# Splitting the expert down product's weights ahead of time and running it as three float32r products

## The reference, cut to what matters

```python
E, TOP_K, H, I = (8, 2, 256, 704)
probs = jax.nn.softmax(x @ gate_w.T, axis=-1)
topk_vals, topk_idx = jax.lax.top_k(probs, TOP_K)
...
g = jnp.einsum('th,eih->tei', x, w1)
u = jnp.einsum('th,eih->tei', x, w3)
a = jax.nn.silu(g) * u
y = jnp.einsum('tei,ehi->teh', a, w2)
out = jnp.einsum('te,teh->th', combine, y)
```

## Time and profile before

| | |
|---|---|
| median of 3 runs | 578.97 us (578.96, 578.97, 583.65) |
| span of the profiled execution | 579.5 us |
| the profiled execution's own time | 581.32 us |
| PE, PEld busy | 88%, 72% of the span |
| DVE, ACT, POOL busy | 65%, 50%, 28% |
| mean granted PE clock | 0.957 of full speed |
| moved by DMA | 47.46 MB, mean 82 GB/s |

### The profile page before, as it was taken

The page is one execution under the profiler, slowest core; times in us unless marked ns, Lnnn a source line. Parts: engine busy times, 40 slices in busy tenths (PEclk is TensorE's granted clock), DMA queues, the critical chain, the costliest instruction groups (busy, mean ns, idle before and its releaser), DMA issues. The chain is left out here.

```text
span 579.5 us, 9940 instructions
## 1 busy us (share of the span) xinstructions
PE 512.8 (88%) x3274; PEld 418.7 (72%) x3275; DVE 377.1 (65%) x964; ACT 287.1 (50%) x528; POOL 161.3 (28%) x221
## 2 busy tenths in 40 slices
PE   1996988999999989889989999628999999999994
PEld 1645776787787866667777777517888888898883
DVE  4896666737554545777777878356677766666661
ACT  1477432314402345555566566326666666666651
POOL 3703423932012202433222202110322222222222
PEclk9998989999999995899899999958999999999999
DMA  9997002000000019500000003941211222222111
GB/s 339 393 335 226 2 1 74 0 1 0 1 16 22 1 38 418 221 18 30 29 10 19 29 1 117 402 123 28 32 28 34 36 36 36 36 36 36 27 17 20
DMA packets 25780, 47.46 MB, mean 82 GB/s; under 512 B 2192, under 2 KB 21136, under 8 KB 25360
## 3 DMA queue, kind: packets, MB, share of 16 engines
q1 hardware_dynamic: 21232, 41.35, 19.8%
q0 software_dynamic: 4080, 5.15, 5.8%
q10 hardware_dynamic: 432, 0.49, 0.3%
HBM read 32.01 MB, written 14.98 MB: 81 GB/s over the span
## 5 line engine op out<-in xcount | busy, mean ns | idle before, releaser
L1609 PE MATMUL ps<-split,xsT 128*128 128x352 f32 x552 | 95.5, 329 | 0.8 <-DVE split L1251 0.8
L1609 PEld LDWEIGHTS ps<-split,xsT 128*128 128x128 f32 x552 | 89.4, 192 | 1.0 <-issue 1.0
L1251 DVE TENSOR_TENSOR split<-early,split 128x1408 fp32r<-128x1408 f32 x46 | 72.6, 1618 | 1.9 <-ACT split L788 1.9
L1631 PE MATMUL ps<-mid,work 128*128 (+1 forms) x276 | 67.9, 387 | 0.8 <-ACT work L777 0.8
L788 ACT CAST split<-early 128x1408 fp32r x46 | 62.6, 1365 | 0.8 <-issue 0.8
L1631 PEld LDWEIGHTS ps<-mid,work 128*128 128x128 f32 (+1 forms) x276 | 49.6, 189 | 13.5 <-issue 8.7
L1232 DVE TENSOR_TENSOR work<-work,ps 128x704 f32<-128x704 f32 x23 | 20.4, 889 | 56.4 <-PE ps L1609 56.4
L1121 DVE TENSOR_REDUCE nmax<-ps 128x1 f32<-128x128 f32 (+7 forms) x64 | 45.4, 751 | 7.5 <-PE ps L1515 7.4
L568 POOL TENSOR_TENSOR rstd<-mhalf 128x1 f32<-128x1 f32 x23 | 11.4, 495 | 138.2 <-ACT work L784 138.2
L1526 PE MATMUL ps<-cst,work 128*128 128x128 f32 x216 | 35.7, 294 | 4.8 <-DVE work L1129 2.8
L733 ACT COPY work<-ps 128x128 f32<-128x128 f32 (+7 forms) x32 | 20.6, 643 | 33.9 <-PE ps L1526 33.8
(11 more groups left out here) (250 smaller groups left out, 1129.9 us busy)
## 6 DMA issues: line engine op xcount, KB each, us to landing
early<-m_w SPq DMA_DIRECT2D x16, 704.0 KB, 10.2
expert_in<-pad SPq DMA_DIRECT2D x8, 1040.0 KB, 12.6
mid<-m_w SPq DMA_DIRECT2D x8, 640.0 KB, 8.3
work<-expert_in SPq DMA_DIRECT2D x23, 130.0 KB, 2.5
early<-factors SPq DMA_DIRECT2D x1, 2048.0 KB, 12.2
early<-wq SPq DMA_DIRECT2D x1, 2048.0 KB, 16.6
mid<-f_w SPq DMA_DIRECT2D x1, 2048.0 KB, 21.0
rows<-x_in SPq DMA_DIRECT2D x2, 512.0 KB, 5.1
```

The source lines that it names most:

```text
L1251: V.tensor_tensor(lo, (ew1, ew3)[w][:, bass.ds(e, 1), :], hi.bitcast(F32), ALU.subtract).then_inc(s_wlo[w], 1)
L1609: last = mm(ps[:, 2 * w + a, 0:IH], xsT[px][b][:, k, :], split_w[w][pw][:, k, a * IH:(a + 1) * IH], start=(k == 0 and px == pw), stop=(k = ...
L1631: last = mm(ps[:, 6, 0:D], eaT[0:w, b, c, :], we[0:w, c, :], start=(c == 0), stop=(c == IB - 1))
```

## The change

**Down product.** It becomes three float32r products: 18 of 256 columns instead of 6 float32 ones. Its activation is split behind the transposes: ACT rounds 512 and 256 columns into `eaT[0]`, DVE subtracts them into `eaT[1]`, both in one buffer for all tiles.

**Weights `w2`.** They are split once for all experts in the feed-forward stage, in 16 pieces of 128 x 768. A piece is loaded into one of four buffers in `mid`, rounded by ACT, subtracted by DVE, and both parts are stored to DRAM. `W2_AT_BLOCK` and `W2_BETWEEN` say behind which block a piece is handled. At the end of attention the high parts of all experts are loaded into `mid` as before; the low part of one expert (768 KB) is loaded for each tile, two buffers.

**Up product.** The 1408 columns of `w1` and `w3` lie side by side and are made in products of 512, 512 and 384 columns, 18 a tile instead of 24. The semaphore on which silu and the rounding of the next `w1` wait comes after the second of the three blocks (it came after the first half), that for DVE's product after the third.

**Padding.** The weights get 768 rows, zeros in the last 64, and the activation 64 zero columns; all six chunks are full.

```diff
+W2_COLS = IB * D // 2
+W2_BUFS = 4
+W2_PIECES = 2 * E
...
+        W2_AT_BLOCK = {2: 0, 3: 1, 4: 2, 5: 3, 6: 4, 7: 5, 8: 10, 9: 11, 10: 12, 13: 13, 14: 14, 15: 15}
+        W2_BETWEEN = (6, 7, 8, 9)
...
+            def store_w2_piece(p):
+                e, half = divmod(p, 2)
+                sp.wait_ge(s_w2lo, p + 1)
+                for d, part in zip(w2_split_d, (w2_hi, w2_lo)):
+                    sp.dma_start(d[e * P:(e + 1) * P, half * W2_COLS:(half + 1) * W2_COLS],
+                                 part[p % W2_BUFS].bitcast(F32)).then_inc(s_w2st[p % W2_BUFS], 16)
+
+            sp.wait_ge(s_mo, TT)
+            for p in range(W2_BUFS):
+                load_w2_piece(p)
...
+            for p in range(W2_PIECES):
+                store_w2_piece(p)
+                if p + W2_BUFS < W2_PIECES:
+                    sp.wait_ge(s_w2st[p % W2_BUFS], 32 * (p // W2_BUFS + 1))
+                    load_w2_piece(p + W2_BUFS)
...
+            def load_ahead(i, b, first=False):
+                sp.wait_ge(s_ext, i + 1)
+                sp.wait_ge(s_dest, i + 1)
+                load_slots(i + 2, b)
+                if not first:
+                    sp.wait_ge(s_ey, i - 1)
+                    load_w2_lo(i, b)
...
+            def w2_piece_hi(p):
+                act.wait_ge(s_w2ld[p % W2_BUFS], 16 * (p // W2_BUFS + 1))
+                nc.scalar.copy(w2_hi[p % W2_BUFS], w2_raw[p % W2_BUFS]).then_inc(s_w2hi, 1)
+
...
                 if q == FB:
                     feature_major(PH_FFN, 1, C_LN2)
+                    for p in W2_BETWEEN:
+                        w2_piece_hi(p)
...
             feature_major(PH_ATT, 0)
+            for b in range(W2_BUFS):
+                act.wait_ge(s_w2st[b], 32 * W2_PIECES // W2_BUFS)
...
-                nc.scalar.copy(eaT[:, b, 0:4, :].rearrange("p a b -> p (a b)"), ps[:, 4, :]).then_inc(s_eaa, 1)
+                for c, w in ((0, 4), (4, 2)):
+                    nc.scalar.copy(eaT[0][:, c:c + w, :].rearrange("p a b -> p (a b)"),
+                                   ps[:, 4 + c // 4, 0:w * P]).then_inc(s_eah, 1)
...
+            def w2_piece_lo(p):
+                dve.wait_ge(s_w2hi, p + 1)
+                b = p % W2_BUFS
+                V.tensor_tensor(w2_lo[b], w2_raw[b], w2_hi[b].bitcast(F32), ALU.subtract).then_inc(s_w2lo, 1)
...
-            ffn_residual(range(GT))
+            for p in W2_BETWEEN[:2]:
+                w2_piece_lo(p)
+            for t in range(GT):
+                ffn_residual(range(t, t + 1))
+                if t < 2:
+                    w2_piece_lo(W2_BETWEEN[2 + t])
...
-                V.tensor_copy(eaT[:, b, 4, :], ps[:, 5, 0:P])
-                V.tensor_copy(eaT[0:ILAST, b, 5, :], ps[0:ILAST, 5, P:2 * P]).then_inc(s_ead, 1)
-
+                for n, (c, w) in enumerate(((0, 4), (4, 2))):
+                    dve.wait_ge(s_eah, 2 * i + n + 1)
+                    hi, lo = (a[:, c:c + w, :].rearrange("p a b -> p (a b)") for a in eaT)
+                    last = V.tensor_tensor(lo, ps[:, 4 + c // 4, 0:w * P], hi.bitcast(F32), ALU.subtract)
+                last.then_inc(s_eal, 1)
...
+                for a in range(3):
+                    if a < 2:
+                        pe.wait_ge(s_wlo[a], i + 1)
+                    c0, c1 = a * 512, min((a + 1) * 512, 2 * I)
+                    for k in range(KD):
+                        for px, pw in PARTS:
+                            last = mm(up_flat[:, c0:c1], xsT[px][b][:, k, :], split_w[pw][:, k, c0:c1],
+                                      start=(k == 0 and px == pw), stop=(k == KD - 1 and px == 1))
+                    if a:
+                        last.then_inc((s_eg, s_eu)[a - 1], 1)
...
+                pe.wait_ge(s_eah, 2 * i + 2)
+                pe.wait_ge(s_ew2lo[b], 8 * (i - b) + 16)
+                pe.wait_ge(s_eal, i + 1)
...
-                for c in range(IB):
-                    w = min(P, I - c * P)
-                    last = mm(ps[:, 6, 0:D], eaT[0:w, b, c, :], we[0:w, c, :], start=(c == 0), stop=(c == IB - 1))
+                we_split = (we, ew2_lo[b].rearrange("p (c n) -> p c n", c=IB))
+                for px, pw in PARTS:
+                    for c in range(IB):
+                        last = mm(ps[:, 6, 0:D], eaT[px][:, c, :], we_split[pw][:, c, :],
+                                  start=(c == 0 and px == pw), stop=(c == IB - 1 and px == 1))
```

More of the change, by code:

```diff
@@ L231, in build @@
         split_t = sb("split", 4 * KD * I, F32R)
-        split_w = [[view(split_t, (w * 2 + part) * KD * I, KD, I) for part in range(2)] for w in range(2)]
+        split_w = [view(split_t, part * 2 * KD * I, KD, 2 * I) for part in range(2)]
         xsT_t = sb("xsT", 4 * D, F32R)
@@ L1099, in _ @@
             normalise(PH_FAC, x, 1)
+            for b in range(W2_BUFS):
+                dve.wait_ge(s_w2st[b], 32 * W2_PIECES // W2_BUFS)
             for q in range(FILLS):
```

114 lines of the change are left out of this document (67 added, 47 removed).

## The result

The changed kernel takes **592.31 us** in the median of four runs (589.87 to 593.9); the kernel before has 579.14 (four runs, 578.96 to 583.65). The ratio is 1.0167 with a 95% interval of 1.0126 to 1.0207: slower by 1.3 to 2.1%. The median lies outside the forecast's 1% and 0.3 us above the upper end of the range (592). By the ratio it is 586.4 to 591.1 us where before has 579.14, which is inside the range; the two medians alone give 1.0227, above that interval, so the size of the loss is known to some 3 us only. The first rival, a slow ring with 588 us, is what happened.

The account below looks back on a forecast made before the run. PE was taken to bound the loop before, a chain through DVE and ACT after; 579.5 - 10.4 (loop) + 9.2 (ring) + 1.0 (clock) = 579.3, about 579 us, no change. Range 568 to 592 us; within 1% (573.2 to 584.8) had 0.45.

Parts of the forecast that it names:

- The first rival: Feed-forward stage: reads and stores in one queue hold each other up, cycle 5.5 us, 588 us; 0.33 together with an ungained loop.
- The loop: Tile loop: rounds fall from 7.64 to 7.1 us, a gain of 10.8 us over the 20 full rounds.
- a chain of 7.08 us: Tile loop: second up block, silu, rounding of the next w1, both low parts and handovers bound a round, not PE's 6.88.
- The two handovers of 0.1: Tile loop: estimated 0.1 us each for two handovers between DVE, ACT and PE; bound 7.3 us a round at 0.2 each.
- DVE's room: Tile loop: DVE has about 6.1 us of work in a 7.1 us round, so splitting the activation hides.
- Transfers in the loop and at the end of attention: A tile's low weights take 1.9 us plus a fixed part, the extra high weights 1.5 us; both hide.
- The pieces' own work: Feed-forward stage: a piece takes DVE 0.93 to 1.4 us and ACT 0.81, costed at nothing inside blocks of 2.8 us.
- The cycle of the ring: Feed-forward stage: SP's two stores, wait and load take 4.6 us a piece, bounds 3.8 and 5.4; second group 9.2 us later.
- the load's share: Feed-forward stage: the load issued just before, 0.94 to 1.2 us, may add from nothing to all of itself to each cycle.
- The steps behind the cycle: Feed-forward stage: late pieces delay the additions, 6 us per us of cycle; from 4.9 piece 14 leads, 11 us per us.
- The clock: Feed-forward stage: PE's wait of about 5 us for piece 7 lowers its clock, costing 1 us, bounds 0 and 3.
- PE at 1.2 GHz in the second group: Feed-forward stage: a sign named beforehand that would show the forecast wrong, PE running at reduced clock there.

Follow-up runs that it names:

- e6: Against the kernel before: e1 with the up product back in 24 products of 352 columns and semaphores at its halves; ratio 0.9724, rounds 6.85 us.
- e9: The change with SP storing the next piece before waiting, pieces respread, and the up product in 352 columns with semaphores at the halves; ratio to before 0.9738.
- e3: The change with only the low parts stored, one store a piece, high parts left unrounded; ratio to the kernel before 1.0009.
- e5: The change with the loads of pieces 4 to 15 issued by ACT, in another queue than SP's stores; ratio to the kernel before 1.0234.
- e4: The change with DVE's low parts of pieces 6 to 9 moved behind the first group's additions, statistics and normalised rows; ratio to before 1.0156.
- e2: The change with SP issuing the stores of piece p + 1 before waiting for those of piece p; ratio to the kernel before 0.9929.
- e7: The kernel before with the padding alone: 768 weight rows, six full chunks, still float32 products; ratio 0.9899, rounds 7.31 us.
- e11: The change's serial ring with 8 pieces of 1536 columns in two buffers, handled at other blocks; one run 582.52 us, before 583.27.
- e1: The change with only piece 0 loaded and split, its parts stored to all 16 places without waits between; ratio to the kernel before 0.9863.

## Why the forecast missed and what of it held

**The loop held.** Forecast was a chain of 7.08 us and rounds of 7.1, against 7.13; a gain of 10.8 us over 20 rounds, against 10.3. Each link is in the trace: from the second up block to silu 495.68 - 494.00 = 1.68 (1.41 + 0.24 forecast), 0.72 to the rounding (0.71), the rounding 1.37, both low parts 3.16 (3.15), the idle time ahead of the second block 0.24 (some 0.2). The two handovers of 0.1 and the 0.03 for a restarting PE had no row behind them; the trace has 497.91 - 497.77 = 0.14 from ACT's rounding to DVE's low part and 0.05 from there to PE. e6 shows that this chain, not PE, is the bound, and that PE's own round is 6.85 (6.88 forecast). The down product came to 2.13 us (2.14 forecast). DVE's room held as well: the activation's low part made no wait except at the last tile, where PE stood 2.13 us for it (0.82 before); the shorter last product was to pay for that and the tail came out 0.9 longer. The clock explains this, not the order: the last down product ran mostly at half clock, behind that wait.

```profile
580.02 1.57 PE L1719 MATMUL ps<-expert_w,eaT 128*128 x6 [2.13 <-DVE eaT L1352]
```

Its 18 products took 3.91 us from there, at a mean clock of 0.57, where the 12 of before took 3.05; in the profiled execution of e9 they took 2.42 at full clock behind a wait of 2.03, and the tail was 1.2 us shorter than before's (20.7 against 21.9).

**Transfers in the loop and at the end of attention held:** 4.3 us to landing for a low part, and no wait of PE for them. (The high weights are 512 KB more than before, 0.52 MB and not 0.6.)

**The pieces' own work held, with a caveat.** 0.93 to 1.4 for DVE, measured 1.49 to 1.50 for the first five, 0.94 to 0.96 for the others, and 1.12 on the mean; 0.81 for ACT, measured 0.84. e9 shows that it can be hidden, down to 0.4 us, but only once the pieces are ready in time.

**The cycle of the ring is the term that failed.** It was 4.6, "the middle" of 3.8 and 5.4, and is 5.55, above the upper bound. The lower part was close: 3.3 to 3.7 for the pair and 0.5 for an issue, measured 3.32 where no load runs and 0.38. The mis-sized term is the load's share: it was let in at 0 to 1.2 us, its bytes alone, and costs 1.85 in the change, 1.83 in e3 and 1.9 in e5. Choosing the middle made it worse: of the two ends, the upper had all three transfers in flight together, which is what the code does in every cycle, and the lower assumed that one of them was free. The rest of the 20 us followed from this term, at 6 to 11 us for each us of the cycle.

**The steps behind the cycle held, the last one by luck.** With 5.5 in place of 4.6 my formulas give piece 7's load at 107.1 + 22 - 0.5 = 128.6 (measured 128.21), piece 9's at 139.6 (139.13), and piece 14 rounded at 171.1 (171.90). But piece 14 is not what held the last silu:

```profile
172.83 0.60 ACT L763 ACTIVATE work<-ps 128x512 f32<-128x512 f32 x1 [0.92 <-PE ps L1521]
```

ACT waited for PE there. What led was piece 12: DVE handled it at 159.87, the product behind it came at 161.88, PE started again at 162.61 and then made the remaining blocks without a wait, 3.40 us of that time at half clock, which is 1.7 us lost. That this ended 0.9 us behind piece 14 is why the rival's delay of 17.1 + 2 for the clock comes so near to the 19.2 in the trace. (The two paths cross at c = 5.0 by the prediction's own terms, not 4.9.) It was right that from about 5 us on late pieces of the second group lead, and not the hold of the additions: e4 takes that hold away and gains 1.1 us at most. The rival's 588 us is the 588.8 that the ratio gives; the profiled span grew by 11.1 where the rival has 8.7, and the 2.4 between them are the 1.3 ahead of the loop, the 0.9 at the tail, and tenths.

**The clock** was put at 1 us with bounds of 0 and 3. PE had 13.6 us at half clock in the stage. The first 10.2 of them stood under waits for DVE, as argued: the next additions came at 144.46, when piece 9 let them, and PE stood another 2.92 us for DVE ahead of 151.18. The last 3.4 did not, and cost 1.7. Of the signs named beforehand as speaking against the forecast, "PE at 1.2 GHz in the second group" came true. The Trainium skill, "TensorE: Matmul & The Clock Gate", "Part 1: The HAM clock gate", says that an idle TensorE loses clock; PE's 8.95 us wait had it in its second half, and in e2's profiled execution, with no wait of PE in the stage above 1.9, the clock stayed at 1.00, so the trace agrees.

**A fixed part and a rate do not give the cycle either.** The Trainium skill, "DMA: Bandwidth & Descriptors", "Anatomy of one DMA — SWDGE (gpsimd) path", has about 2.0 us and 436 GB/s, for another queue than this. The estimate by it was c = 4.3 without the load; with all three transfers of a cycle in it, an estimate by it is 2.0 + 1.18 MB / 436 GB/s = 4.7 us. Both are under the measured 5.55, while its 3.8 for the pair of stores is above the measured 3.32: here the fixed part is smaller, about 1.4 us, and what is missing is the load's share beside the stores.

## What to carry to other kernels

Where a program stages data through DRAM in a ring of buffers, write down what is in flight while a landing is waited for. One that waits for each store before it issues the next pays the fixed part of a transfer in every cycle, and here a load in flight slowed the stores from whichever queue it came; issuing the next piece's stores ahead of the wait was worth 15 us of the stage here (12.6 to 13.8 us of the whole by the ratios), and no engine's work changed. A piece of work that is small and "fits into every block" still costs as much as its data is late, because the engine works in order: put it where the engine waits anyway, and see first that the data is there.

Undo one part of a change at a time before judging it: here the padding alone was worth 1.0%, the wide product nothing (and 0.28 us a round less than nothing together with the rest), and the split down product 1.6% of time (e9 against e7, with some 0.6 either way) once the ring stopped taking it back.

## What the runs showed of the hardware

- A pair of 393 KB stores is through in 3.32 us when alone and in 5.25 us when a load of 393 KB starts with it in another queue (e5); in the same queue the load's issue and its share add 2.2 us (the change). One store alone takes 2.35 us (e3), two of double size 5.15 (e11).
- Stores of 393 KB back to back: one each 0.98 us, 400 GB/s, each 4.1 us from issue to landing (e1).
- A load in flight beside the stores adds 1.8 to 1.9 us for 393 KB (the change, e3, e5) and 3.5 for 786 KB (e11), about twice its bytes at 417 GB/s; no run shows why.
- A float32 product of 256 columns with 128 rows shows as two records of 0.2155 us, 2.59 us for six chunks; with a last chunk of 64 rows the weight loads stood idle for 0.33 us on either side of it, and the padding made the down product 0.29 us shorter (e7).
- DVE's subtraction of 768 columns takes 1.49 to 1.50 us in the change between 105 and 118 us, where POOL is busy in all of the time, and 0.96 from 131 on, where POOL is idle; in e9 it is 1.36 and 1.23 at the end of the first group. I take POOL's work for the cause, but no run separates it.
